# A GRU scan behind a causal depthwise convolution: start-up loads, the bias memset and the first turned rounds rearranged

## The reference

```
x = x + causal_depthwise_conv(x, w)        # 16 taps along time
h = cond                                    # initial state, [16, 512]
for t in range(256):
    gi = x[:, t] @ W_ih + b_ih              # W_ih, W_hh: [512, 1536], split into r, z, n
    gh = h @ W_hh + b_hh
    r = sigmoid(i_r + h_r); z = sigmoid(i_z + h_z)
    n = tanh(i_n + r * h_n)
    h = (1 - z) * n + z * h
    out[:, t] = x[:, t] + h
```

## Time and profile before

| | us |
|---|---|
| median of 3 executions | 1033.27 |
| all three | 1036.97, 1033.27, 1033.23 |
| the profiled execution's own time | 1037.14 |
| its span, first to last instruction | 1035.3 |
| PE busy in the span | 1022.1 |

### The profile page before, as it was taken

One profiled execution on the slowest core, in us unless ns is written; L12 is line 12 of the kernel. 1 busy time (PEld: TensorE's weight loads), 2 busy tenths in 40 slices (PEclk: granted clock), 3 DMA queues, 4 the chain that ended last, 5 costly groups with the idle time before them and its releaser, 6 DMA issues.

```text
span 1035.3 us, 58526 instructions
## 1 busy us (share of the span) xinstructions
PE 1022.1 (99%) x25148; PEld 1003.5 (97%) x25148; DVE 791.6 (76%) x2598; ACT 396.9 (38%) x1812; POOL 239.8 (23%) x782
## 2 busy tenths in 40 slices
PE   8999999999999999999999999999999999999997
PEld 5889999999999999999999999999999999999996
DVE  8558888888888888888888877777777765555555
ACT  3333333433433433433333333333343343343342
POOL 3212222222222222222222222222222222222222
PEclk9999999999999999999999999999999999999999
DMA  8665321000010100101000010100100000000000
GB/s 281 65 79 66 48 24 49 4 25 28 3 49 4 37 16 14 39 3 49 4 24 24 3 44 3 34 14 5 42 4 23 4 19 9 4 24 3 24 14 13
DMA packets 102786, 31.58 MB, mean 31 GB/s; under 512 B 86016, under 2 KB 100992, under 8 KB 102528
## 3 DMA queue, kind: packets, MB, share of 16 engines
q1 hardware_dynamic: 102096, 27.73, 12.3%
q10 hardware_dynamic: 432, 0.11, 0.1%
HBM read 19.35 MB, written 8.49 MB: 27 GB/s over the span
## 4 chain that ended last, share of the span: by engine, by line
PE 96%; issue 2%; POOL 1%; DVE 0%; DMA 0%; ACT 0%; POOLq 0%; DVEq 0%
PE pg L302 64%; PE pg L292 31%; PE pcv L317 1%; POOL tz L255 1%; DMA cnd<-cond 0%; DVE hp L504 0%; DVE gn L483 0%; POOL nzh L268 0%; DVE gt L479 0%; POOLq L42 0%; ACT rz L411 0%; DVE an L491 0%; POOL nzh L254 0%; POOL zcp L253 0%; POOL rz L252 0%
## 5 line engine op out<-in xcount | busy, mean ns | idle before, releaser
L302 PE MATMUL pg<-whh,hp 128*32 128x192 f32 x16384 | 730.8, 327 | 7.3 <-DVE gn L474 3.7
L302 PEld LDWEIGHTS pg<-whh,hp 128*32 128x32 f32 x16384 | 666.2, 110 | 16.5 <-DVE gn L474 4.0
L292 PE MATMUL pg<-wih,x 128*32 128x192 f32 x8192 | 395.4, 326 | 0.0
L268 POOL TENSOR_TENSOR nzh<-rz,hp 128x32 f32<-128x32 f32 x512 | 158.4, 309 | 790.2 <-ACT rz L411 790.2
L292 PEld LDWEIGHTS pg<-wih,x 128*32 128x32 f32 x8192 | 337.1, 110 | 3.8
L411 ACT ACTIVATE rz<-gt 128x64 f32<-128x64 f32 x512 | 136.1, 266 | 502.4 <-DVE gt L479 474.9
L479 DVE STREAM_TRANSPOSE gt<-pg 128x128 f32<-128x128 f32 x512 | 161.8, 316 | 108.2 <-PE pg L302 98.2
L504 DVE TENSOR_TENSOR_SCAN hp<-zcp,nzh 128x96 f32<-128x96 f32 x512 | 172.7, 337 | 77.4 <-ACT nzh L416 77.4
L491 DVE TENSOR_TENSOR_SCAN an<-rz,gn 128x64 f32<-128x64 f32 x512 | 149.2, 291 | 52.3 <-ACT rz L411 51.9
L416 ACT ACTIVATE nzh<-an 128x32 f32<-128x32 f32 x512 | 120.6, 235 | 126.0 <-DVE an L491 126.0
L456 DVE SCALAR_TENSOR_TENSOR x<-xb,cnd,x 128x1024 f32<-128x1024 f32 (+1 forms) x120 | 133.1, 1109 | 0.0
(11 more groups left out here) (38 smaller groups left out, 71.8 us busy)
## 6 DMA issues: line engine op xcount, KB each, us to landing
out<-x SPq DMA_DIRECT2D x60, 128.0 KB, 2.1
xw<-x SPq DMA_DIRECT2D x32, 128.0 KB, 4.5
wih<-w_ih SPq DMA_DIRECT2D x4, 768.0 KB, 7.9
xb<-x SPq DMA_DIRECT2D x16, 158.0 KB, 2.3
tz<-x SPq DMA_DIRECT2D x16, 158.0 KB, 2.3
whh<-w_hh SPq DMA_DIRECT2D x4, 512.0 KB, 12.7
xb<-x SPq DMA_DIRECT2D x16, 126.0 KB, 2.1
whh<-w_hh SPq DMA_DIRECT2D x4, 256.0 KB, 11.4
```

The lines of the kernel that those rows point to most:

```text
L268: pool.tensor_tensor(nzh[:, f, ::2, :, 1], chunks(rz[:, f, 1, :, 1]), h_of(t - 1, slice(f * CH, (f + 1) * CH)), ALU.mult).then_inc(s_zh[f], 1)
L292: i = pe.matmul(pg[m % Q][f][D * j:D * (j + 1), RZ:END], x1_of(c, 2 * m, 2 * m + 2), wih[:, c, :, :].rearrange("p (g k) (j d) -> p j g k d ...
L302: i = pe.matmul(pg[t // 2 % Q][f][D * j:D * (j + 1), 0:IN], hp[:, t % 2, 2 * c + 1 - t % 2:2 * c + 3 - t % 2, :, 1].rearrange("p u b -> p ...
```

## The change

- POOL waits for both bias transposes (`s_bc` at 2) before its memset of `tz`.
- `whh` is `[P, C, 4F]`. Each part c of W_hh comes in one transfer of 768 KB into `whh[:, c, F:4F]` in the order r, z, n. n's columns of all four parts come once more (1 MB, `s_whn`) into `whh[:, :, 0:F]`. Step 0 uses `recur_first`, which reads r and z (128 columns) and the first copy of n (64 columns) by two matmuls; the later steps use `recur` on `whh[:, c, 0:3F]`, as before, behind a wait of PE for `s_whn`.
- SP waits for all four parts and for `s_whn` before it enters the loop over t, whose first DMAs are the band loads.
- WARM is 6 instead of 20. In step 0 four matmuls of zeros follow part 1 and three follow part 2 (`IDLE`).
- `ROUNDS[(0, 0)]` is (6, 8) instead of (7, 8): 8 turned rounds at the end of step 6 and 8 at the end of step 7, instead of 16 at the end of step 7.
- One pair of `xw` tiles instead of two; SP waits for `s_cv` before it loads the second pair's windows into them.

```diff
-WARM = 20
+WARM = 6
+IDLE = {1: 4, 2: 3}
...
-        xw = [[sb(f"xw{p}{l}", [P, P // 2, 2, B]) for l in range(H)] for p in range(PAIRS)]
+        xw = [sb(f"xw{l}", [P, P // 2, 2, B]) for l in range(H)]
-        whh = sb("whh", [P, C, 3 * F])
+        whh = sb("whh", [P, C, 4 * F])
...
-        ROUNDS = {(0, 0): (7, 8), (0, 1): (10, 11), (1, 0): (17, 21), (1, 1): (30, 34)}
+        ROUNDS = {(0, 0): (6, 8), (0, 1): (10, 11), (1, 0): (17, 21), (1, 1): (30, 34)}
...
+                if p and q == 0:
+                    sp.wait_ge(s_cv, l + 1)
...
-                sp.dma_start(whh[:, c, 0:F], w_hh[:, c, 2 * F:]).then_inc(s_whh[c], 16)
-                sp.dma_start(whh[:, c, F:], w_hh[:, c, 0:2 * F]).then_inc(s_whh[c], 16)
+                sp.dma_start(whh[:, c, F:], w_hh[:, c, :]).then_inc(s_whh[c], 16)
+            sp.dma_start(whh[:, :, 0:F], w_hh[:, :, 2 * F:]).then_inc(s_whn, 16)
+            for c in range(C):
+                sp.wait_ge(s_whh[c], 16)
+            sp.wait_ge(s_whn, 16)
             for t in range(T):
...
+            pool.wait_ge(s_bc, H)
             pool.memset(tz[:, :, :, :], 0.0).then_inc(s_band, 1)
...
+            def recur_first(f, c):
+
+                hh = hp[:, 0, 2 * c + 1:2 * c + 3, :, 1].rearrange("p u b -> p (u b)")
+                for j in range(J):
+                    o = pg[0][f][D * j:D * (j + 1), :]
+                    pe.matmul(o[:, RZ:IN], hh,
+                              whh[:, c, F:3 * F].rearrange("p (g j f n) -> p j f g n", g=2, j=J, f=H)[:, j, f],
+                              start=False, stop=True, skip_group_check=True)
+                    i = pe.matmul(o[:, 0:RZ], hh,
+                                  whh[:, c, 3 * F:].rearrange("p (j f n) -> p j f n", j=J, f=H)[:, j, f],
+                                  start=False, stop=True, skip_group_check=True)
+                return i
...
             for c in range(C):
-                pe.wait_ge(s_whh[c], 32)
+                pe.wait_ge(s_whh[c], 16)
                 for f in range(H):
-                    i = recur(0, f, c)
+                    i = recur_first(f, c)
                     if c == C - 1:
                         i.then_inc(s_gh[f], 1)
+                for _ in range(IDLE.get(c, 0)):
+                    pe.matmul(pcv[:, 0:512], zeros[:, 0:P], zeros[:, :], start=True, stop=True)
             for c in range(C):
                 product(2, 0, c)
+            pe.wait_ge(s_whn, 16)
             for t in range(1, T):
```

More of the change, by code:

```diff
@@ L88, in build @@
         s_whh = [sem(f"s_whh{c}") for c in range(C)]
+        s_whn = sem("s_whn")
         s_xw = [halves(f"s_xw{p}") for p in range(PAIRS)]
@@ L184, in load @@
                 c, e = l * CH + g // 2, g % 2
-                sp.dma_start(xw[p][l][W2 * g:W2 * (g + 1), :, i, :],
+                if p and q == 0:
+                    sp.wait_ge(s_cv, l + 1)
+                sp.dma_start(xw[l][W2 * g:W2 * (g + 1), :, i, :],
                              x[:, c, t * B:(t + W2) * B].rearrange("(p e) (w b) -> e w p b", e=2, b=B)[e]
@@ L303, in recur @@
                                   hp[:, t % 2, 2 * c + 1 - t % 2:2 * c + 3 - t % 2, :, 1].rearrange("p u b -> p (u b)"),
-                                  whh[:, c, :].rearrange("p (g j f n) -> p j f g n", g=3, j=J, f=H)[:, j, f],
+                                  whh[:, c, 0:3 * F].rearrange("p (g j f n) -> p j f g n", g=3, j=J, f=H)[:, j, f],
+                                  start=False, stop=True, skip_group_check=True)
[9 more added lines that the diff above has]
+                                  whh[:, c, 3 * F:].rearrange("p (j f n) -> p j f n", j=J, f=H)[:, j, f],
                                   start=False, stop=True, skip_group_check=True)
@@ L317, in turn @@
                     i = pe.matmul(pcv[D * j:D * (j + 1), r * G * K:(r + 1) * G * K],
-                                  xw[p][l][:, j * K + r, :, :].rearrange("p i b -> p (i b)"),
+                                  xw[l][:, j * K + r, :, :].rearrange("p i b -> p (i b)"),
                                   tz[:, l, j * K + r, :], start=True, stop=True)
```

## The result

The changed kernel takes 1038.49 us in the median (6 executions, 1038.20 to 1039.22); the kernel before, measured beside it, 1033.72. The ratio is 1.0041, with a 95% interval of 1.0027 to 1.0054. The forecast was 1037.8 in 1032.0 to 1040.7. Measured once more (12 executions) the change gave 1038.68 and a ratio of 1.0028 (1.0013 to 1.0043).

What follows compares the result with a forecast made beforehand. PE, busy 99%, was taken to bound the kernel. Step 8 comes +1.15 us later, plus 1.7 for the clock: +2.85; with 1.68 the median cannot regain, 1033.27 becomes 1037.8 (+0.44%), range 1032.0 to 1040.7.

Steps and rivals of the forecast that it cites:

- Memset behind the bias transposes: At the start, bias copies no longer wait for the 6.9 us memset: `first` at 5.85, products' transposes at 17.0, not 23.0.
- Rival C: At the start, the memset holds `first` up to 12; step 1 near 29.6, time 1034.5; chance 0.10.
- W_hh and step 1: Step 0 follows W_hh's parts to 23.3, then PE waits for `s_whn`; step 1 at 26.0, gain 3.4 us.
- The load queue: All 16 loads start at 26.0, at 1.75 us intervals, landing by 55.15; the turned rounds are asked for at 49.4.
- The stand: PE waits 5.75 us at the end of step 6 for the loads that the turned rounds need.
- Rival B: Loads come quicker, at a pace of 1.45 us; PE stands 1.25 and keeps its clock; 1031.6; chance 0.20.
- The clock: After PE's wait at the end of step 6 the clock falls, costing 1.7 us (bounds 0.4 and 3.4).
- The gap in step 8: The stall at step 8 behind 256 short PE instructions goes when 128 stand in a row: -1.17 us.
- From the profiled execution to the median: Of 3.87 us between profiled execution and median, 1.68 may already be absent in the median: 1033.27 + 2.85 + 1.68.
- those two stalls: PE's wait before step 0 with its lower clock, 1.68 us lost, and the stall at step 8, 1.17 us.
- Rival A: Median runs have neither the step 0 nor the step 8 stall: 1039.0, or 1040.7 if the clock stays low; chance 0.25.

Runs made afterwards that it cites:

- the filled stand: Changed kernel with 22 matmuls of zeros at the end of step 6, ahead of the turned rounds, filling PE's wait there; 1038.58 us, ratio 1.0034.
- the lower-level trace: The kernel before, unchanged, profiled once more for an execution that kept the clock; 1033.47 us, span 1031.7.

## Why the prediction was right, and where it was not

- **Memset behind the bias transposes: right.** `first` at 5.84 (5.85 predicted), the products' transposes at 17.03 (17.0). Rival C is out: `first` ran beside the memset at 0.68 us, as after it (0.63). The Trainium skill's rule for two SBUF inputs (SBUF, State Buffer, "Who interferes with whom") holds here, and the trace of the change agrees with it: from `first` to the products' transposes DVE took 17.03 - 5.84 = 11.19 us, against 11.15 behind the memset.
- **W_hh and step 1: a little off.** 25.23 instead of 26.0. The four parts landed by 22.5 and not 23.3, and the second copy 2.7 us later, as reckoned. The reason given for an earlier landing, no band behind them, is not it: in the run without SP's waits, with bands behind them, the last part is used from 22.55 too. What brought them earlier is open.
- **The load queue: right, 1 us too late.** The landing was 53.99 instead of 55.15. The first band took 4.2 us instead of 2.9, and the 15 intervals were (53.99 - 29.64) / 15 = 1.62 us instead of 1.75. The stand was 5.14 instead of 5.75. Rival B's pace of 1.45 did not come: the same count gives 1.66 in the second trace of the change and 1.70 with the rounds at (7, 8).
- **The clock: right.** 1.7 predicted, 1.6 by the filled stand.
- **The gap in step 8: right that it goes, its cause not shown.** It is absent in both traces of the change. But the number of short instructions is not the whole of it: the run with rounds at (7, 8) has 256 of them and no gap, the run with the filled stand 128 and a gap of 0.34 us. In all, step 8 starts at 61.30 where the prediction's working gives 60.85 + 1.7 = 62.55.
- **From the profiled execution to the median: wrong in its cause, and this hid the rest.** On its own time the working gives 1040.0 and the profiled execution of the change took 1038.41, 1.6 less. To carry the sum over, I took 1.68 of the 3.87 us between the levels as a start that the change could no longer mend, for the clock in step 0. The sentence "I know no place but those two stalls where the start can vary so much" is the step that failed. The whole 3.74 us lie ahead of step 1, in the race at the memset, which I had described from the same rows without seeing that it could go the other way. So the carry should have been 3.87 and not 1.68. Two errors of opposite sign, 2.2 us too little here and 1.6 too much on the profiled execution, leave 0.6; the last 0.1 is the change's median over its profiled execution. That the forecast lies within 0.7 us of the result is in part luck. Rival A came nearest in time (1039.0), and its mechanism is half right: in the lower level the stall before step 0 is absent, but step 8's gap is there, 0.53 us.

Against the lower-level trace the 5.0 us of span (1031.7 to 1036.7) come out as -0.4 at step 1, +5.1 stand, +1.7 clock, -0.8 for the gap of step 8, -0.7 at step 10 (6.38 to 5.69 us from step to step), and 0.1 left.

## What to carry to other kernels

Count the transfers ahead of a wait and their pace before moving the wait earlier or their start later: here 16 small-run loads at 1.6 to 1.75 us each fixed the time of the turned rounds, whatever the start gained. When the executions of a kernel lie on two levels, profile one of each before costing a change: a start-up edit may only repair what the median does not suffer from.

## What the runs showed of the hardware

- A DVE copy that became ready at 3.13 us passed between POOL's back-to-back memsets; ready at 3.35 and 3.75 it was held until the last one's end, 7.6 and 7.3 us later.
- 256 short PE instructions in a row (16 rounds) left gaps with no visible wait of 0.5 to 1.8 us in some places and none in others: at step 8 in four traces (0.96, 0.53, 1.13 and 0.91 us) and not in the one with the rounds at (7, 8) on the changed kernel. With 128 in a row there was none at step 8 in the two traces of the change and in six others, and 0.34 us in one, that of the filled stand. The cause is open.
- The clock fell 5.0 us into the stand in one trace of the change and 2.2 us into it in the other (48.81 to 50.98), and cost 1.8 and 1.9 us: from `an` on DVE (L515) in step 6 to the same in step 7 it is 59.03 - 47.31 = 11.72 and 59.35 - 47.28 = 12.07 us, of which 3.90, 0.89 for half the rounds, and the stand of 5.14 or 5.34 are taken off.
